# A two-layer kernel on one core: all 16 shared tiles ahead of the routed ones in the first feed-forward layer, batch 1's steps later in attention's prologue

## The chip, the core and the metric

The kernel runs on one core of a Trainium2 chip. That core has a matrix engine (PE in the rows; PEld is its weight load, which overlaps its matmuls), a vector engine (DVE), a scalar engine (ACT), a general engine (POOL) and an engine that mostly starts transfers (SP). "SPq" and "ACTq" in a row are the queues from which SP and ACT start transfers. The metric is the device time of one execution in microseconds (us), as a median of runs.

## What is computed

The input is 2 batches of 1024 tokens with 128 values each. Three residual layers follow one another: a feed-forward layer with a shared expert and seven routed ones of which each token takes two, causal attention with 16 heads of 8 values, and the same feed-forward layer again.

```python
x = x + 0.5 * ffn(layernorm(x))
x = x + attn(layernorm(x))
x = x + 0.5 * ffn(layernorm(x))

def ffn(x):                                     # hidden 352, 7 routed experts
    logits = x @ wr.T + rb
    probs = softmax(logits)
    scores, idx = top_k(probs, 2)
    scores = scores / scores.sum(-1)
    out = expert(x, sg, su, sd)                 # shared
    for e in range(7):
        out = out + w[..., e:e+1] * expert(x, rg[e], ru[e], rd[e])
    return out                                  # expert: silu(x @ g.T) * (x @ u.T), then d

def attn(x):                                    # v = x @ w_v + v_b
    q = (x @ w_q + q_b) @ w_k.T + k_b
    k = x                                       # split into 16 heads of 8
    p = softmax(mask(q @ k.T / sqrt(8)))
    return (p @ v) @ c_proj_w + c_proj_b
```

## The kernel before

**Units of work.** Tokens lie in 16 tiles of 128, and four tiles are a chunk of 512: chunks 0 and 1 are batch 0, chunks 2 and 3 are batch 1. A feed-forward layer does 54 jobs (`NQ`): 16 shared tiles, and 38 routed tiles (`NJ`) whose rows have been sorted by expert. A job takes one step of PE for `up` (L899 to L901: two products of 352 columns, three matmuls each), a step later the transposes of its activations (L919), a step later `down` (L933). ACT does the silu (L1000) and the copy of the transposes (L1008), DVE the product (L1043) and the result (L1079 for a routed tile, L1081 for a shared one).

**The order of jobs** is `JOBS` from `BEFORE`: in the first layer (f = 0) 13 shared tiles, the 38 routed ones, then the last 3 shared ones. POOL sorts: 32 indirect transfers (L1174) write token rows to their places in memory, the first 16 for batch 0 and the next 16 for batch 1, with a short pause (L1184) behind each. SP then loads sorted tiles into the chip (L1260). Routed tiles come in batches (`BATCHES`: tiles 0-1, 2-5, 6-9, 10-11, 12-13, then fours); PE transposes a batch (L953) at the step that `batch_at` names, two steps ahead of its first job where it can. Routed tiles 0 to 9 hold rows of batch 0 alone, so they wait for the first 16 sorts; batch 3 (tiles 10-11) waits for all 32. POOL writes each routed tile's result back to memory (L1197), and after tile 21 batch 0's results are complete and after tile 37 batch 1's.

**Between the layers**, chunk by chunk: load the results (L1271), weigh and add them (ACT L1114 and DVE L1093, L1104 for batch 0; ACT L1126 and POOL L1138 for batch 1), statistics on DVE (L504, L507), four small instructions on POOL for the scale (L515 to L521), the normed rows `z` on ACT (L540), their transposes on PE (L573), a high part on ACT (L579) and a low part on DVE (L585), then the query product `q` on PE (L1508 to L1510 with wq), ACT (L1563, L1565) and DVE (L1571), and the value product `v` on PE (the same lines with wv), ACT (L1543) and POOL (L1553). For batch 0 these steps are placed at steps of the first layer by four hand-written tables: `FRONT_PE`, `BETWEEN_ACT`, `BEHIND_ACT` and `BEHIND_DVE`. "Front" is at the start of the engine's step, "behind" at its end. So `44: (("n_tr", 0),)` puts chunk 0's transposes at the head of PE's step 44. For batch 1 they are placed in attention's prologue by `SECOND_PE` and `SECOND_DVE`, at numbers of ring entries.

**Attention** works on 8 groups of four heads, 4 for each batch. Queries and keys go out to memory in a stacked form (SP L1578) and come back group by group, 5 transfers for one group (L1928 queries, L1936 keys). For each group there are ring entries: 38 blocks of scores (L1605, a mask at L1608 on the diagonal) whose maxima DVE takes (L1757), then a short chain on DVE (L1761, L1763, L1765) and two transposes of the maxima (L1628), which SP puts into the queries (L1949). After that come the exponentials: scores (L1648), exp on ACT (L1816), a mask on POOL (L1863), and the product with the values (L1677). The prologue is the 54 ring entries of `RING_PROLOGUE`: the 38 blocks of group 0, one of group 1, the two transposes, then 13 of group 1. From entry 45 on, score units for the exponentials run among them. Every engine takes its instructions strictly in the order in which they are written, so a wait holds up all that stands behind it on that engine; a ring entry on PE may run four ahead of DVE.

Three key buffers are used in turn. Buffer 2 is cleared by SP (L1421) from memory before group 2 is loaded into it (L1928, L1936); group 2's first block stands in PE's first loop body behind the 24 last blocks of group 1.

The last part of SP's program for the prologue reads in its order (L1977 to L1986):

```python
    for c in range(NCH // 2, NCH):
        keys_sp(K, c)
    for c in range(NCH // 2, NCH):
        queries_sp(K, c)
    rows_load(K, 0, 0, 0, RING_PROLOGUE.index(("mrow", 0, 0)))
    for c in range(NCH // 2, NCH):
        e.wait_ge(K.k_st[c], 16 * 3)
        e.wait_ge(K.q_st[c], 16 * 3)
    keys_clear(K, 2)
    e.wait_ge(K.cleared, keys_cleared(1))
```

## Time and profile before

| what | us |
|---|---|
| median of 3 runs | 570.33 |
| lowest and highest of them | 570.11 and 571.10 |
| the profiled execution, its own time | 571.84 |
| its span, first to last instruction | 570.0 |
| PE busy in it | 521.1 (91%) |
| DVE busy | 388.5 (68%) |
| ACT busy | 319.8 (56%) |
| POOL busy | 272.1 (48%) |

The profiled execution took 571.84 us, of which 570.0 lie between its first and its last instruction. In its trace the first feed-forward layer ends and attention's prologue begins at 162.84 us; the first scores for an exponential start at 199.86 us; the loop over the groups ends near 402 us, and the second feed-forward layer fills the rest. A share of busy time is a mean over stages that are bound by different things, so each stage is read by itself, by what PE waited for last.

### The profile page before, as it was taken

What the parts mean: (1) busy time and instruction counts of PE and PEld (TensorE: products, weight loads), DVE (VectorE), ACT (ScalarE), POOL (GpSimd) and SP (SyncE); (2) the same over time, 40 slices, a digit from 0 to 9 for tenths busy, and PEclk for the clock granted to TensorE, in tenths of its full rate; (3) what the DMA queues carried; (4) which work ended last, traced back from release to release, by engine and by line L of the source; (5) the groups of instructions that cost most, each with busy time, mean ns of one, the idle gap of its engine ahead of it and who ended that gap; (6) DMA issues with size and microseconds to landing.
All of it is one profiled execution on the core that took longest, in us unless ns stands there. A gap on an engine that the chain in (4) does not pass through costs nothing.

```text
span 570.0 us, 11374 instructions
## 1 busy us (share of the span) xinstructions
PE 521.1 (91%) x3574; PEld 406.0 (71%) x3574; DVE 388.5 (68%) x1013; ACT 319.8 (56%) x678; POOL 272.1 (48%) x417
## 2 busy tenths in 40 slices
PE   5985969999996799999999999999999889889995
PEld 2884969998954465656666666565746889889995
DVE  5694635557367888887979888888555775445744
ACT  4552424457444276776767677677776444434643
POOL 8299887667356711212120303030318888854540
PEclk9899789999996899999999999999999999999999
DMA  8922424132861581505050505020001031431414
GB/s 283 294 67 50 111 77 120 45 107 81 242 183 56 170 190 35 173 2 175 2 174 1 176 0 176 1 102 2 2 2 33 31 91 43 118 92 34 125 50 121
DMA packets 41384, 54.65 MB, mean 96 GB/s; under 512 B 6064, under 2 KB 32176, under 8 KB 40560
## 3 DMA queue, kind: packets, MB, share of 16 engines
q1 hardware_dynamic: 32528, 42.70, 26.4%
q0 software_dynamic: 4480, 9.25, 4.9%
q10 hardware_dynamic: 4320, 1.98, 1.3%
q8 instruction: 32, 0.52, 0.4%
q14 instruction: 24, 0.20, 0.1%
HBM read 34.03 MB, written 28.00 MB: 109 GB/s over the span
## 4 chain that ended last, share of the span: by engine, by line
PE 57%; issue 18%; POOL 10%; DMA 6%; DVE 4%; SPq 2%; ACT 2%; ACTq 1%; another core or an unknown queue 1%; POOLq 0%; DVEq 0%
PE psum L1605 11%; PE psum L1648 11%; PE psum L1677 10%; PE psum L933 6%; POOL z_rows L1174 6%; PE psum L919 3%; PE psum L901 3%; PE psum L899 3%; PE psum L900 3%; PE psum L1608 2%; POOL idle L1184 2%; DMA b_p<-in_attn_c_proj_b 2%; DMA yc<-y_rows 1%; DMA y_rows<-ys,to_row 1%; PE psum L1633 1%
## 5 line engine op out<-in xcount | busy, mean ns | idle before, releaser
L1757 DVE TENSOR_REDUCE mxp<-psum 128x1 f32<-128x512 f32 (+3 forms) x304 | 179.0, 654 | 32.9 <-PE psum L1605 32.1
L1816 ACT ACTIVATE probs<-psum 128x512 f32<-128x512 f32 (+1 forms) x304 | 154.9, 578 | 39.8 <-PE psum L1648 37.2
L1863 POOL TENSOR_SCALAR_AFFINE_SELECT probs<-probs 128x512 f32<-128x512 f32 x64 | 40.0, 635 | 174.2 <-ACT probs L1816 174.2
L1648 PE MATMUL psum<-queries,keys 128*128 128x512 f32 (+3 forms) x384 | 122.5, 381 | 0.6 <-DMA queries<-m_rows 0.3
L1605 PE MATMUL psum<-keys,queries 128*128 128x512 f32 (+1 forms) x304 | 116.1, 417 | 2.9 <-DVE mxp L1757 2.4
L1000 ACT ACTIVATE silu<-psum 128x352 f32<-128x352 f32 x107 | 49.6, 463 | 99.5 <-PE psum L901 62.6
L1197 POOL DMA_INDIRECT y_rows<-ys,to_row x76 | 74.3, 977 | 59.1 <-DVE ys L1079 35.4
L1043 DVE TENSOR_TENSOR act<-silu,psum 128x352 f32<-128x352 f32 x107 | 55.6, 519 | 68.0 <-ACT silu L1000 41.7
L933 PE MATMUL psum<-wall_f,at 128*128 (+1 forms) x648 | 92.2, 279 | 2.7 <-DVE x L1081 1.8
L1648 PEld LDWEIGHTS psum<-queries,keys 128*128 128x128 f32 x384 | 66.8, 191 | 26.8 <-ACT probs L1816 12.6
L933 PEld LDWEIGHTS psum<-wall_f,at 128*128 128x128 f32 x648 | 82.1, 194 | 4.1 <-ACT at L1008 2.3
L1605 PEld LDWEIGHTS psum<-keys,queries 128*128 128x128 f32 x304 | 58.1, 194 | 18.1 <-DVE mxp L1757 7.8
L1677 PE MATMUL psum<-probs,vg 128*32 128x512 f32 (+3 forms) x768 | 69.8, 491 | 0.4 <-POOL probs L1863 0.4
L919 PE MATMUL psum<-ident,act 128*128 128x128 f32 x324 | 54.7, 278 | 5.9 <-DVE act L1043 4.4
L899 PE MATMUL psum<-wall,zs_h 128*128 x152 | 56.9, 374 | 1.0 <-issue 1.0
L1008 ACT COPY at<-psum 128x384 f32<-128x384 f32 x108 | 51.3, 475 | 11.0 <-PE psum L919 9.7
L900 PE MATMUL psum<-wall,zs_h 128*128 x152 | 50.4, 331 | 0.0
L901 PE MATMUL psum<-wall,zs_l 128*128 x152 | 50.2, 330 | 0.0
L919 PEld LDWEIGHTS psum<-ident,act 128*128 128x128 f32 x324 | 41.0, 142 | 12.3 <-DVE act L1043 8.2
L1677 PEld LDWEIGHTS psum<-probs,vg 128*32 128x32 f32 x768 | 21.1, 109 | 35.4 <-issue 22.9
L1174 POOL DMA_INDIRECT z_rows<-zrow,slots x32 | 34.4, 1076 | 15.9 <-DVE slots L750 10.5
L1174 POOL DMA_INDIRECT z_rows<-zrow_late,slots x32 | 31.2, 975 | 5.8 <-issue 5.8
(240 smaller groups left out, 732.4 us busy)
## 6 DMA issues: line engine op xcount, KB each, us to landing
z_rows<-q_stack SPq DMA_DIRECT2D x12, 682.5 KB, 5.6
keys<-k_stack SPq DMA_DIRECT2D x32, 128.0 KB, 5.9
queries<-q_stack SPq DMA_DIRECT2D x8, 512.0 KB, 5.3
zg_early<-z_rows SPq DMA_DIRECT2D x44, 65.0 KB
yc<-y_rows SPq DMA_DIRECT2D x10, 256.0 KB, 4.0
zg_late<-z_rows SPq DMA_DIRECT2D x32, 65.0 KB
k_stack<-zt_h SPq DMA_DIRECT2D x8, 256.0 KB, 2.9
q_stack<-q_h SPq DMA_DIRECT2D x8, 256.0 KB, 3.7
```

Source lines behind the costliest of these rows:

```text
L899: e.matmul(dst, zh, weight(K.wall, base, hi, HID), start=True, stop=False)
L900: e.matmul(dst, zh, weight(K.wall, base, lo, HID), start=False, stop=False)
L901: ins = e.matmul(dst, zl, weight(K.wall, base, hi, HID), start=False, stop=True)
L919: ins = e.transpose(bank(K, at_bank(f, q))[:, k * P:(k + 1) * P], K.act[:, q % 2, k * P:(k + 1) * P], K.ident[:, :])
L933: ins = e.matmul(bank(K, Y_BANK)[:, 0:EMB], K.at[:, q % 2, k * P:(k + 1) * P], weight(K.wall_f, base, DN + k * EMB, EMB), start=(k == 0), ...
L1174: e.indirect_dma_start(K.z_dram[f], bass.IndirectOffsetOnAxis(ap=K.slots[:, g:g + 1], axis=0), K.zrow[f][:, t, :], None).then_inc(K.z_sc[t ...
L1197: e.indirect_dma_start(K.y_dram[f], bass.IndirectOffsetOnAxis(ap=K.to_row[:, j:j + 1], axis=0), K.ys[:, j % RING_Y, :], None).then_inc(K.y ...
L1605: ins = e.matmul(dst, K.queries[u][:, i * P:(i + 1) * P], K.keys[u][:, heads[0]:heads[-1] + 1, k0 * P:(k0 + nb) * P], start=True, stop=Tru ...
L1648: ins = e.matmul(slot(K, u, d, n)[:, m * (q1 - q0):(m + 1) * (q1 - q0)], K.keys[v][:, j, kt * P:(kt + 1) * P], K.queries[v][:, q0:q1], sta ...
L1677: ins = e.matmul(bank(K, O_BANK)[32 * j:32 * j + 32, q0 - half * CHUNK:q1 - half * CHUNK], K.vg[:, kt, j, :], probs_of(K, n)[:, j, :], sta ...
L1757: e.tensor_reduce(K.mxp[:, heads[0]:heads[-1] + 1, i, which], scores, AX.X, ALU.max).then_inc(K.A["taken"], 1)
L1816: e.activation(probs_of(K, product)[:, heads[0]:heads[-1] + 1, :], src, ACT.Exp, scale=SCALE).then_inc(K.A["ex"], 1)
```

## The change

The functions are the same ones, in another order, with a few waits and banks that follow from it.

- **Jobs of the first layer.** All 16 shared tiles come first, the 38 routed ones behind them. `batch_at` now transposes batch 3 (routed tiles 10-11) one step ahead of its first job, not two. The second layer's jobs stay as they are.
- **Batch 0's steps.** Mixing, statistics, transposes and queries move three steps down the tables, so they stand at the same routed tile as before; the exceptions are chunk 1's transposes (step 47 to 49), its query product (48 to 50) and ACT's and DVE's part of it. The normed rows of chunks 0 and 1 are made by DVE (steps 44 and 47, "behind"), where ACT made them. Values of chunks 0 and 1 go from steps 50 and 51 to entries 0 and 2 of the prologue.
- **Batch 1's steps** go to later entries of the prologue: transposes of chunk 2 from entry 19 to 25, of chunk 3 and the queries of chunk 2 from 24 to 30, queries of chunk 3 from 29 to 35, values from 30 and 32 to 36 and 38.
- **Transfers.** SP stores the queries of chunk 1 in two parts, the first four heads (all that group 0 needs) first, loads group 0, then stores the other twelve. Keys of batch 1 are stored from ACT's queue. SP's stores of the queries of batch 1 come behind `rows_load` of group 0.
- **POOL.** The four additions of the projection's bias (L2060) leave the place before attention's loop: two come ahead of `v_bias_pool(0)`, two go into the first loop bodies.

```diff
-BEFORE = (13, 11)
+BEFORE = (TT, 11)
-ONE_AT_AGAIN = (43, NQ)
+ONE_AT_AGAIN = (46, NQ)
-        if step == BEFORE[f] + j - (min(b, 2) if f == 0 else 1 if j == WHOLE else 2):
+        if step == BEFORE[f] + j - min(2 if f else b, 1 if j == WHOLE else 2):
-    return c != 1 if k == 0 else k == 1 or c == 2
+    return c != 1 if k == 0 else c >= 2 if k == 1 else c == 2
 def v_pe(K, c):
     if c == 0:
-        e.wait_ge(K.A["qf"], 1)
+        e.wait_ge(K.A["qf"], 2)
     elif c == 1:
-        e.wait_ge(K.A["qf"], 2)
+        e.wait_ge(K.FF[0]["yev"], NQ)
-SECOND_PE = {19: (("n_tr", 2),), 24: (("n_tr", 3), ("q", 2)), 29: (("q", 3),), 30: (("v", 2),), 32: (("v", 3),)}
-SECOND_DVE = {13: (("n_stats", 2),), 16: (("n_stats", 3),), 20: (("n_lo", 2),), 26: (("n_lo", 3),)}
+SECOND_PE = {0: (("v", 0),), 2: (("v", 1),), 25: (("n_tr", 2),), 30: (("n_tr", 3), ("q", 2)), 35: (("q", 3),), 36: (("v", 2),),
+             38: (("v", 3),)}
+SECOND_DVE = {18: (("n_stats", 2),), 21: (("n_stats", 3),), 26: (("n_lo", 2),), 32: (("n_lo", 3),)}
 def attn_pool(K):
+            if (p, u) in ((0, 1), (0, 2)):
+                proj_bias_pool(K, u + 1)
 def attn_sp(K):
-    for c in range(NCH // 2):
-        keys_sp(K, c)
-        queries_sp(K, c)
+    keys_store(K, e, 0)
+    queries_sp(K, 0)
+    keys_store(K, e, 1)
+    queries_sp(K, 1, (0, 4))
...
     keys_load(K, 0, 0, 0)
-    for c in range(NCH // 2):
-        e.wait_ge(K.q_st[c], 16 * 3)
+    e.wait_ge(K.q_st[0], 16 * 3)
+    e.wait_ge(K.q_first, 16 * 3)
+    queries_load(K, 0, 0, 0)
+    queries_sp(K, 1, (4, HEADS))
     e.wait_ge(K.FF[0]["mix"], 4)
-    queries_load(K, 0, 0, 0)
     keys_load(K, 0, 0, 1)
+    e.wait_ge(K.q_st[1], 16 * 3)
     queries_load(K, 0, 0, 1)
-    for c in range(NCH // 2, NCH):
-        keys_sp(K, c)
+    rows_load(K, 0, 0, 0, RING_PROLOGUE.index(("mrow", 0, 0)))
     for c in range(NCH // 2, NCH):
         queries_sp(K, c)
-    rows_load(K, 0, 0, 0, RING_PROLOGUE.index(("mrow", 0, 0)))
-FRONT_PE = {10: (("places", 1),), 44: (("n_tr", 0),), 45: (("q", 0),), 47: (("n_tr", 1),), 48: (("q", 1),),
-            50: (("v", 0),), 51: (("v", 1),)}
+FRONT_PE = {10: (("places", 1),), 47: (("n_tr", 0),), 48: (("q", 0),), 49: (("n_tr", 1),), 50: (("q", 1),)}
         @block.scalar
+            v_act(K, 0)
+            v_act(K, 1)
             weigh_both_act(K, 2)
...
             q_act(K, 2)
+            keys_store(K, e, 2)
             q_act(K, 3)
+            keys_store(K, e, 3)
         @block.gpsimd
+            e.wait_ge(K.NS[1]["z"], 2)
+            proj_bias_pool(K, 0)
+            proj_bias_pool(K, 1)
             v_bias_pool(K, 0)
             v_bias_pool(K, 1)
...
-            proj_bias_pool(K)
             attn_pool(K)
```

How instructions stand at three places, before and after. Lines of the changed kernel are numbered 1 to 4 higher here for the same statement (L1079 has become L1080, L1757 has become L1760).

DVE near the end of the first layer, where chunk 1 has been mixed (`x<-x,yc`); `act` is the product of a job, `ys` a routed result, `stats` the statistics of chunk 1. Before:

```order
L1093 SCALAR_TENSOR_TENSOR x<-yc,w,x 128x128 x4
L1104 TENSOR_TENSOR x<-x,yc 128x512
L1043 TENSOR_TENSOR act<-silu,psum 128x352
L1079 COPY ys<-psum 128x128
L504 BN_STATS stats<-x 128x6 x4
L507 BN_AGGR mv<-stats 128x2 x4
```

After:

```order
L1094 SCALAR_TENSOR_TENSOR x<-yc,w,x 128x128 x4
L1105 TENSOR_TENSOR x<-x,yc 128x512
L553 TENSOR_SCALAR z<-x,mv,rstd 128x128 x4
L1044 TENSOR_TENSOR act<-silu,psum 128x352
L1080 COPY ys<-psum 128x128
L505 BN_STATS stats<-x 128x6 x4
L508 BN_AGGR mv<-stats 128x2 x4
```

The four instructions that make chunk 0's normed rows `z` now stand between the mixing and the next job's product.

SP in attention's prologue; `q_stack` and `k_stack` are the stacked queries and keys in memory, `m_rows` the maxima of group 0, `keys<-q_stack` the clearing of key buffer 2, and the rows behind it group 2's load. Before:

```order
L1578 DMA k_stack<-zt_l 16x8x512
L1578 DMA k_stack<-zt_h 16x8x512
L1578 DMA q_stack<-q_h 16x8x512 x2
L1578 DMA q_stack<-q_l 16x8x512
L1578 DMA q_stack<-q_h 16x8x512 x2
L1578 DMA q_stack<-q_l 16x8x512
L1949 DMA queries<-m_rows 4x8x128 x2
L1421 DMA keys<-q_stack 32x4096 x4
L1928 DMA queries<-q_stack 128x1024
L1936 DMA keys<-k_stack 32x1024 x4
```

After:

```order
L1942 DMA keys<-k_stack 32x1024 x4
L1934 DMA queries<-q_stack 128x1024
L1955 DMA queries<-m_rows 4x8x128 x2
L1579 DMA q_stack<-q_h 16x8x512 x2
L1579 DMA q_stack<-q_l 16x8x512
L1579 DMA q_stack<-q_h 16x8x512 x2
L1579 DMA q_stack<-q_l 16x8x512
L1422 DMA keys<-q_stack 32x4096 x4
L1934 DMA queries<-q_stack 128x1024
L1942 DMA keys<-k_stack 32x1024 x4
```

The four rows of stores of batch 1's queries stood ahead of `m_rows` and now stand between it and the clearing; those of batch 1's keys are gone from SP.

PE in the prologue around the transposes of chunk 2 (the first `ident,z`) and of chunk 3 (the second), with the query product of chunk 2 (`wq`). Before:

```order
L1605 MATMUL psum<-keys,queries 128x512 x2
L573 MATMUL psum<-ident,z 128x128 x4
L1605 MATMUL psum<-keys,queries 128x512 x4
L1608 MATMUL psum<-ident_b,mask_b 128x512
L1605 MATMUL psum<-keys,queries 128x512
L573 MATMUL psum<-ident,z 128x128 x4
L1508 MATMUL psum<-zt_h,wq_h 128x512
L1509 MATMUL psum<-zt_l,wq_h 128x512
L1510 MATMUL psum<-zt_h,wq_l 128x512
```

After:

```order
L1607 MATMUL psum<-keys,queries 128x512 x2
L574 MATMUL psum<-ident,z 128x128 x4
L1607 MATMUL psum<-keys,queries 128x512 x5
L1610 MATMUL psum<-ident_b,mask_b 128x512
L574 MATMUL psum<-ident,z 128x128 x4
L1509 MATMUL psum<-zt_h,wq_h 128x512
L1510 MATMUL psum<-zt_l,wq_h 128x512
L1511 MATMUL psum<-zt_h,wq_l 128x512
```

The pieces read alike; 6 more ring entries (`keys,queries`) stand ahead of the first of them, 25 instead of 19.

## Rows read from the trace of the kernel before

**Rows 1.** The page's second part: 40 equal slices of the span, 14.25 us each.
```profile
PE   5985969999996799999999999999999889889995
```
**Rows 2.** Waits of PE up to 260 us: total, times, longest.
```profile
PE psum L1628 <- DVE mm_hl L1765: 3.5, 1, 3.5
```
**Rows 3.** Busy time by stage: stretch, its length, each engine, then PEclk, DMA share, GB/s.
```profile
57.90:77.40 19.50, 19.44 (x128) 19.05 (x128) 12.71 (x42) 8.06 (x19) 17.52 (x26) 0.86 0.34 85
163.00:200.00 37.00, 26.54 (x96) 15.69 (x96) 31.93 (x69) 14.22 (x33) 21.73 (x31) 0.82 0.40 121
```
**Rows 4.** Timeline: start, length, engine, line, work [idle before and its releaser]; first wait.
```profile
51.13 0.96 POOL L1174 DMA_INDIRECT z_rows<-zrow,slots  x1 [0.17 <-issue]
...
56.44 0.50 PE L953 MATMUL psum<-ident,zg_early 128*128 128x128 f32 x2 [4.90 <-DMA zg_early<-z_rows]
```
**Rows 5.** The same timeline, second wait, and two successive jobs at full clock.
```profile
82.05 0.66 PE L953 MATMUL psum<-ident,zg_early 128*128 128x128 f32 x2 [4.67 <-DMA zg_early<-z_rows]
...
95.16 0.41 PE L899 MATMUL psum<-wall,zs_h 128*128 x1
...
97.12 0.41 PE L899 MATMUL psum<-wall,zs_h 128*128 x1
```
**Rows 6.** Timeline of PE behind the step of chunk 1's mixing; L552's four instructions on DVE.
```profile
132.94 0.55 PE L919 MATMUL psum<-ident,act 128*128 128x128 f32 x3 [0.66 <-DVE act L1043]
...
L552 DVE TENSOR_SCALAR zrow<-x,mv,rstd x4: 314/342/343, 10.8 to 11.5; 128x128 f32<-128x128 f32 x4
```
**Rows 7.** Timeline of the last jobs and of group 0's load, with that load's landing.
```profile
148.07 0.69 DVE L1571 TENSOR_TENSOR q_l<-q_f,q_h 128x512 fp32r<-128x512 f32 x1 [0.44 <-ACT q_h L1565]
149.51 0.31 PE L1508 MATMUL psum<-wv_h,zt_h 128*128 128x128 f32 x1
150.88 0.38 PE L899 MATMUL psum<-wall,zs_h 128*128 x1
154.95 0.34 SPq L1928 DMA_DIRECT2D queries<-q_stack  x1
...
162.84 0.48 PE L1605 MATMUL psum<-keys,queries 128*128 128x512 f32 x1
DMA to landing us min/median/max: 4.4/4.4/4.4
```
**Rows 8.** Timeline of batch 1's results, from the last routed tile to chunk 2's transposes.
```profile
158.39 0.29 DVE L1079 COPY ys<-psum 128x128 f32<-128x128 f32 x1
168.73 5.32 POOL L1138 TENSOR_TENSOR x<-x,yc 128x512 f32<-128x512 f32 x4 [5.47 <-ACT yc L1126]
...
177.85 1.09 PE L573 MATMUL psum<-ident,z 128*128 128x128 f32 x4 [3.09 <-issue]
```
**Rows 9.** Prologue: DVE's first maxima, POOL's value biases, the maxima's chain over all groups.
```profile
163.70 7.33 DVE L1757 TENSOR_REDUCE mxp<-psum 128x4 f32<-128x512 f32 x13
...
L1553 POOL TENSOR_TENSOR v_all<-v_all,b_v 128x128 f32<-128x128 f32 x16 | 6.7, 456 | 0.0
L1763 DVE CAST mm_hl<-nmax x8: 180/520/1192, 193.9 to 399.4; 128x32 fp32r<-128x32 f32 x8
L1765 DVE TENSOR_TENSOR mm_hl<-nmax,mm_hl x8: 192/193/1195, 195.1 to 399.7; 128x32 fp32r<-128x32 f32 x8
```
**Rows 10.** Timeline of SP with the times to landing, and group 2's first block on PE.
```profile
188.12 1.24 SPq L1578 DMA_DIRECT2D q_stack<-q_h  x2
...
198.59 1.71 SPq L1421 DMA_DIRECT2D keys<-q_stack  x4
211.03 1.82 SPq L1936 DMA_DIRECT2D keys<-k_stack  x4
q_stack<-q_h SPq DMA_DIRECT2D x8, 256.0 KB, 3.7
keys<-k_stack SPq DMA_DIRECT2D x4, 128.0 KB, 4.9
...
221.86 0.40 PE L1605 MATMUL psum<-keys,queries 128*128 128x512 f32 x1
```

64 lines of the change are left out of this document (32 added, 32 removed).

## The prediction

> **What bounds the kernel now.** Read first PE's line in the 40 slices [rows 1]. From the 15th slice on it stands at 9 through the loop over the groups: there nothing but PE sets the pace, and an earlier start of the loop moves the end by as much. The low digits lie before it: slices 4 and 6 (43 to 57 us and 71 to 86 us) and slices 13 and 14 (171 to 200 us). The change works on just these places, so each is read for what PE waits for last.
>
> In the first layer PE waits twice for sorted rows. It stands idle for 4.90 us before the transposes at 56.44 [rows 4], which wait for SP's load, which waits for the 16th sort, issued by POOL at 51.13. It stands idle for 4.67 us before those at 82.05 [rows 5], which need all 32 sorts. POOL's pace and not PE's sets both moments. What PE does in the meantime is free. Behind the first wait the granted clock is low: 0.86 as a mean from 57.9 to 77.4 us, where PE is busy for 19.44 of 19.50 us [rows 3]; since the clock knows only two levels, 1.2 and 2.4 GHz, some 5 us of that stretch ran at the lower.
>
> In the prologue from 163 to 200 us, PE is busy for 26.5 us of 37 and DVE for 31.9 [rows 3], so DVE's maxima and the chain that brings batch 1's rows share the bound. Two waits of PE show which: 3.09 us before chunk 2's transposes at 177.85 [rows 8], and 3.5 us for the maxima's chain [rows 2].
>
> **Shared tiles first.** A job at full clock takes 1.96 us on PE (97.12 less 95.16, [rows 5]). PE reached the first wait at 56.44 - 4.90 = 51.54. Three more jobs fill it to 57.4, 1 us behind the rows' arrival, so this wait goes entirely, and with it the half clock behind it. About 0.5 us of transposes and 1 us until ACT and DVE have split the rows remain, then come nine jobs (nine, because batch 3's transposes now stand one step later) and eight more transposes: 58.9 + 9 x 1.96 + 0.8 = 77.3 us. That is where PE stood before, at 82.05 - 4.67 = 77.38, with eight routed jobs done. What is late next is therefore the second wait, and I take it unchanged: POOL's 32 sorts depend on nothing that moves. At 82.05 the kernel has done 25 jobs instead of 21. Everything behind is 4 x 1.96 = 7.8 us shorter for PE. The routed tiles are only one job earlier, 2.0 us.
>
> **Values out of the layer.** Twelve matmuls of chunk 0's values take 150.88 - 149.51 = 1.37 us [rows 7], chunk 1's the same: -2.7 us for the layer. They come back in the prologue, chunk 0's ahead of the first ring entry (+1.4), chunk 1's behind the second, under DVE's maxima.
>
> **Rows normed by DVE.** Four instructions on DVE cost 11.5 - 10.8 + 0.34 = 1.1 us [rows 6]. For chunk 0 they stand between the mixing and the next job's product, and just there PE already waits 0.66 us for that product [rows 6]. DVE is late in this step, so I take the whole 1.1 us as a delay of PE; it would be nothing if the results came earlier than I think. For chunk 1 the four stand in a step in which DVE waits for rows anyway: nothing. Taking them off ACT gives PE nothing, as it didn't wait for them. Chunk 1's transposes and queries one step earlier make ACT's and DVE's steps crowded: +0.3, between 0 and 1.
>
> PE ends the layer at 162.84 - 7.8 - 2.7 + 1.1 + 0.3 = 153.7 us.
>
> **Group 0's load.** With chunk 0's values PE is at 155.1 before the first ring entry. The low part of chunk 1's queries was done at 148.07 + 0.69 = 148.76 and the load had landed at 154.95 + 4.4 = 159.35 [rows 7], 10.6 us later; PE came only at 162.84, so it did not see this. Now the queries are earlier by one job, by one step and later by the 1.1 us: 148.76 - 2.0 - 2.0 + 1.1 = 145.9. With the old distance the load lands at 156.5. The first part stores only four of sixteen heads and so should be quicker; keys and queries of group 0 still have to come, so 154.3 is the least I allow. I take 155.5, nearer the upper end than half way since the 4.4 us of the last load remain. The first ring entry moves by 155.5 - 162.84 = -7.3 us.
>
> **Batch 1's chain.** It starts at the last routed result, at 158.39 + 0.29 = 158.68 before. This one now is the last job of the layer, so it ends about 0.5 us behind PE, at 154.2: -4.5 us. From there results go to memory, come back, are weighed, added and normed, and chunk 2's transposes follow at 177.85, 19.2 us later [rows 8]. One thing is added on POOL: the value biases of chunks 0 and 1 (8 instructions, about 3.4 us by [rows 9]) now wait for ACT, whose copies stand behind its wait for the results' store. They end some 0.8 us after the addition at 168.73 - 4.5 = 164.2 could start (nothing if ACT is early, 2 us if late). Chunk 2's transposes: 177.85 - 4.5 + 0.8 = 174.1. Ahead of them stand 25 ring entries instead of 19; DVE took 7.33 us for 13 [rows 9], 0.56 each, and its first one starts 0.9 us behind PE's, at 156.4, so with some 2.5 us of statistics and a wait of 0.8 us for the added rows it has done 25 at 156.4 + 14.1 + 2.5 + 0.8 = 173.8. The chain and the ring now meet at about the same moment, and the 3.09 us of waiting is used up. Before, entry 37 was done about 0.3 us before 193.9 [rows 9], 15.8 us after the transposes; six entries fewer stand between, so 15.8 - 6 x 0.56 = 12.4, and DVE begins the last chain at 186.5 instead of 193.6: -7.1 us.
>
> **The maxima's chain.** Its cast and subtraction took 1.19 and 1.20 us for group 0, against a median of 0.52 and 0.19 over the groups [rows 9], while POOL added the projection's bias beside them, the additions that the change takes away. Their place is taken by value biases of 0.456 us each [rows 9]. The gain lies between 0 and 1.7 us; I take 1.2, nearer the upper end because these instructions are a third as long. The Trainium skill (SBUF — State Buffer, "Who interferes with whom") says that a DVE instruction with two inputs in SBUF, or a cast in a two-port mode, and a POOL instruction exclude each other for a whole instruction; the rows of this chain agree, and by it each of the two would wait for one bias at most, so the gain would be at least 1.19 + 1.20 - 0.52 - 0.19 - 2 x 0.46 = 0.8 us, an estimate. The first scores for an exponential so start at 199.86 - 7.1 - 1.2 = 191.6.
>
> **Stores behind `rows_load`.** Here SP pays. Six stores (two took 1.24 us, so 3.7 in all, and 3.7 to land, [rows 10]) now stand between the maxima's rows and the clearing of key buffer 2, where there was nothing. At least the moving of 1.5 MB remains, which I put at 6.5 us; the delay is 6.5 to 7.4. The clearing took from 198.59 to 210.6, group 2's load lands at 211.03 + 1.4 + 4.9 = 217.3, and PE's first block of group 2 stands at 221.86 [rows 10]: 4.6 us to spare. So PE will wait there for 6.6 - 4.6 = 2.0 us, 0 to 4 with what other transfers do to it. PE bounds the loop, so this is lost in full. The keys' stores on ACT (3.7 us of issuing) end before ACT is needed for exponentials; two bias additions in the loop stand on POOL, which is idle for most of it. Both nothing, or up to 0.5 us together.
>
> **Sum.** 7.1 + 1.2 - 2.0 = 6.3 us off the profiled execution's 571.84. That one lies 1.5 us above the median of the runs, and the change doesn't touch the difference: 570.33 - 6.3 = 564.0 us.
>
> **Rivals.** (a) *Group 2 is not missed.* The stores are partly done before the clearing must start, or the clearing is quicker than 12 us since nothing else runs: 564.0 - 2.0 = 562.0. For it: DMA is mostly idle in these stages (0.40, [rows 3]). (b) *Group 0's load is late*: the queries' chain keeps its 10.6 us and gains only the 2.0 of the routed tiles. First entry at 148.76 - 2.0 + 1.1 + 10.6 = 158.5, a wait of 3.4 us and a half clock behind it. The whole prologue slides by 2 to 3 us: 566.5. (c) *Group 2 costs more*, 5 us instead of 2, as clearing and stores meet: 567. (d) *DVE holds up the layer*: the normed rows wait on DVE for POOL, where the scale stands behind a scatter, and jobs queue behind them. 1.5 us more: 565.5. (e) *The change doesn't do what it says*: rows of the first batch still come after PE. They came at 56.4 and PE comes at 57.4; below 1 us of delay it costs nothing, beyond that one for one, so with rows 2.5 us later than before the time is that of (d). (f) *Slower*: the wait for group 2 grows until it eats everything. PE would stand for so long that the clock falls behind it as it did behind the 4.90 us wait; the eight jobs behind it took 19.5 us [rows 3] where 8 x 1.96 + 0.8 = 16.5 would do, 3.0 more. To come out above 570.33 + 1.1 the wait has to exceed 8.3 + 1.1 - 3.0 = 6.4 us, so group 2's rows must land 4.4 us later than I expect. Clearing and stores would have to stretch each other by 40% of the clearing's 12 us. (g) *Nothing moves*, within 0.2%: the same with a wait of 5 to 6.4 us, or (b) and (c) together.
>
> **How the numbers follow.** Forecast 0.42; (a) 0.18; (b) 0.14; (c) 0.10; (d) with (e) 0.07; (f) 0.05; (g) 0.04. Faster by over 0.2%: 0.91; within 0.2%, about what a measurement can tell from no change: 0.04; slower: 0.05. The range leaves out (f), (g) and the outer half of (b) and (c), and reaches down to (a) with 1.5 us for a chain of batch 1 that is quicker: 560.0 to 568.0 us.
>
> **What would show it.** PE's waits in the first layer: one of about 4.7 us at 82 us instead of two, and no half clock between 58 and 77 us. PE's first ring entry near 155.5 us; if it is at 158, (b). Chunk 2's transposes near 174 with less than 1.5 us of waiting. Cast and subtraction below 1 us each. The first exponential's scores near 191.6. Then a wait of PE for `queries<-q_stack` or `keys<-k_stack` about 22 us later; if it is missing, (a). I would be wrong altogether if the second wait in the first layer grew, since POOL's sorts were slower, or if the loop ran slower than before per group.

## The result, and the profile after

Faster by 0.9%: a median of 566.9 us over 13 runs (564.05 to 569.78) against 571.74 us over 13 runs of the kernel before (569.71 to 574.8), ratio 0.991, 95% interval 0.9884 to 0.9935. The forecast was 564.0 us against a before of 570.33, ratio 0.989. The size is near; half of the reasons are not. The profiled execution of after took 569.66 us (span 567.8; before 571.84 and 570.0). It is one of the slower ones of its kernel: the spans differ by 2.2 us, the medians by 4.8. One run of e11 below, of 1270.4 us, fell in a slow state and is left out of its median. Both kernels' runs spread over some 5 us, so the experiments below are read mainly in their traces, place by place.

The 40 slices of after, to be held against [rows 1]. The 5 in slice 4 has become an 8 and the 6 in slice 6 a 7, slices 13 and 14 (7 and 8) stand where 6 and 7 stood, and a new 7 is in slice 16, inside the loop over the groups. Slices 9, 10 and 12 are an 8 instead of a 9:

```profile
PE   5898879988987897999999999999999889899995
PEclk9899999999976997999999999999999999999998
```

Timeline of PE and DVE in after (start, length, engine, line, work, idle time before and its releaser):

```profile
60.48 0.42 PE L900 MATMUL psum<-wall,zs_h 128*128 x1 [1.66 <-DVE zs_l L1068]
...
82.21 0.41 PE L954 MATMUL psum<-ident,zg_early 128*128 128x128 f32 x2 [2.87 <-DMA zg_early<-z_rows]
...
126.59 0.55 PE L920 MATMUL psum<-ident,act 128*128 128x128 f32 x3 [1.49 <-DVE act L1044]
...
132.93 0.55 PE L920 MATMUL psum<-ident,act 128*128 128x128 f32 x3 [1.64 <-DVE act L1044]
...
154.25 0.31 PE L1509 MATMUL psum<-wv_h,zt_h 128*128 128x128 f32 x1
...
157.16 0.50 PE L1607 MATMUL psum<-keys,queries 128*128 128x512 f32 x1 [1.38 <-DMA queries<-q_stack]
...
161.43 0.69 DVE L1760 TENSOR_REDUCE mxp<-psum 128x4 f32<-128x512 f32 x1 [2.21 <-PE psum L1607]
...
175.99 1.09 PE L574 MATMUL psum<-ident,z 128*128 128x128 f32 x4 [1.23 <-issue]
...
187.94 0.25 DVE L1764 TENSOR_REDUCE nmax<-mxp 128x32 f32<-128x96 f32 x1
188.23 0.18 DVE L1766 CAST mm_hl<-nmax 128x32 fp32r<-128x32 f32 x1
188.45 0.19 DVE L1768 TENSOR_TENSOR mm_hl<-nmax,mm_hl 128x32 fp32r<-128x32 f32 x1
...
218.03 0.77 PE L1607 MATMUL psum<-keys,queries 128*128 128x512 f32 x1 [3.58 <-DMA keys<-k_stack]
```

Read down. The 4.90 us wait of [rows 4] is gone; 1.66 us for the rows' split remain. The second wait ends when it ended before, at 82.21 against 82.05 [rows 5]. The layer ends at 154.25. The first ring entry comes at 157.16 instead of 162.84 [rows 7], the last maxima's chain starts at 187.94 instead of 193.6, and its cast and subtraction take 0.18 and 0.19 us. Then PE stands idle for 3.58 us in front of group 2. Busy time in stretches of after (length, engines, then PEclk, DMA share, GB/s):

```profile
158.00:165.00 7.00, 7.00 (x25) 5.22 (x24) 4.61 (x8) 1.07 (x2) 3.15 (x8) 0.51 0.89 248
172.00:182.00 10.00, 8.11 (x22) 5.61 (x23) 9.02 (x22) 4.53 (x11) 5.03 (x11) 0.50 0.00 0
192.00:196.00 4.00, 3.60 (x17) 2.67 (x18) 3.44 (x7) 3.04 (x7) 1.01 (x2) 1.00 0.94 295
196.00:198.00 2.00, 2.00 (x15) 1.83 (x14) 2.00 (x4) 1.98 (x5) 0.64 (x1) 1.00 0.62 201
216.00:218.00 2.00, 0.00 (x0) 0.00 (x1) 0.19 (x1) 0.00 (x0) 0.00 (x0) 0.55 0.15 35
218.00:222.00 4.00, 3.97 (x10) 2.65 (x10) 2.08 (x3) 1.44 (x4) 0.00 (x0) 0.50 0.00 0
222.00:224.00 2.00, 2.00 (x16) 1.67 (x19) 0.88 (x2) 1.25 (x4) 0.64 (x1) 0.74 0.00 0
```

Here is the new 7 of slice 16: no work from 216 to 218, then half clock until some 223 us. The first row is another half clock that was not foreseen, over the values of chunk 1. The second row's half clock is not new: before has one from 173 to 183 us.

**Places of the balance.** Start times (us) in the profiled executions: end of PE's second wait for sorted rows; end of DVE's copy of the last routed result; first ring entry; chunk 2's transposes; the maxima's chain (`nmax`); the first scores for an exponential; SP's third issue of the maxima's rows (`rows_load`); and the distance between the last two. The kernels e1 to e12 are those of the experiments.

| kernel | 2nd wait ends | last routed | ring entry 1 | chunk 2 | `nmax` | first scores | 3rd rows | distance |
|---|---|---|---|---|---|---|---|---|
| before | 82.1 | 158.68 | 162.84 | 177.85 | 193.62 | 199.86 | 255.8 | 55.9 |
| after | 82.2 | 154.83 | 157.16 | 175.99 | 187.94 | 192.40 | 254.2 | 61.8 |
| after again (e11) | none | 153.63 | 156.01 | 174.59 | 185.42 | 189.90 | 250.7 | 60.8 |
| e1 stores ahead | 83.1 | 155.38 | 158.18 | 177.49 | 188.88 | 195.78 | 253.0 | 57.2 |
| e2 values together | 81.5 | 153.79 | 155.93 | 175.01 | 186.55 | 191.01 | 249.7 | 58.7 |
| e3 shared last | 82.1 | 154.07 | 159.61 | 176.47 | 188.10 | 192.56 | 253.6 | 61.0 |
| e4 norm on ACT | 83.7 | 154.62 | 156.42 | 175.77 | 187.34 | 191.79 | 252.6 | 60.8 |
| e5 stores on ACT | 81.8 | 154.88 | 156.32 | 175.95 | 187.13 | 192.87 | 250.1 | 57.3 |
| e6 e3 and e5 | 81.2 | 151.50 | 157.03 | 173.91 | 185.26 | 192.35 | 249.7 | 57.4 |
| e7 bias back | 80.8 | 153.44 | 155.05 | 174.91 | 185.72 | 190.19 | 250.2 | 60.0 |
| e8 batch 3 later | 81.4 | 156.92 | 157.76 | 177.68 | 188.52 | 193.00 | 254.2 | 61.2 |
| e9 clear split | 82.1 | 154.56 | 156.53 | 175.21 | 187.07 | 191.55 | 249.1 | 57.5 |
| e10 values in layer | 82.0 | 156.57 | 156.38 | 175.50 | 187.43 | 191.91 | 251.2 | 59.3 |
| e12 less behind | 83.6 | 155.85 | 157.02 | 176.57 | 188.29 | 193.39 | 249.7 | 56.3 |

Before to after: 7.5 us are won up to the first scores, 5.9 are lost in the last column, 1.6 are left. In e11, the same kernel, it is 10.0, 4.9 and 5.1, which is nearer to what the medians differ by. The experiments ask what made either number.

Two stretches scatter by themselves. Behind the second wait the clock was at 0.5 for 3 us or more in most executions (before from 80.5 to 87.3 us, after from 83 to 86.5) and not at all in e4, e6 and e11. And every kernel has a half clock around chunk 2's transposes. It lasted some 3 us beyond their start in e7, e8 and e11 and 4.4 to 6.1 us in the other changed kernels; from the transposes to `nmax` it is 10.8 us in those three and 11.2 to 12.0 in the others. So about 1 us in the columns from `nmax` on can be the clock alone.

### The profile page after: what moved, and what is told of

It is laid out like the page before. It is cut to its first block, busy times and chain, and to the rows that moved or that the text cites. A ratio compares the mean times of both kernels' runs of the same rounds, so it can differ in the third digit from the quotient of the medians.

```text
span 567.8 us, 11380 instructions
## 1 busy us (share of the span) xinstructions
PE 521.3 (92%) x3574; PEld 406.8 (72%) x3574; DVE 389.0 (69%) x1021; ACT 317.0 (56%) x670; POOL 272.2 (48%) x413
## 4 chain that ended last, share of the span: by engine, by line
PE 56%; issue 20%; DMA 10%; DVE 6%; SPq 5%; ACT 1%; ACTq 1%; DVEq 0%
PE psum L1607 11%; PE psum L1650 10%; PE psum L1679 9%; PE psum L934 6%; PE psum L920 3%; PE psum L902 3%; PE psum L900 3%; PE psum L901 3%; PE psum L1610 2%; DMA b_p<-in_attn_c_proj_b 2%; DVE mxp L1760 2%; DMA keys<-q_stack 2%; SPq L1261 2%; DMA q_stack<-q_l 1%; SPq L1254 1%
## 5 line engine op out<-in xcount | busy, mean ns | idle before, releaser
L1760 DVE TENSOR_REDUCE mxp<-psum 128x1 f32<-128x512 f32 (+3 forms) x304 | 179.3, 656 | 41.5 <-PE psum L1607 33.6
L1607 PE MATMUL psum<-keys,queries 128*128 128x512 f32 (+1 forms) x304 | 117.5, 423 | 6.9 <-DMA keys<-k_stack 3.6
L934 PEld LDWEIGHTS psum<-wall_f,at 128*128 128x128 f32 x648 | 81.5, 193 | 3.7 <-ACT at L1009 1.7
L1607 PEld LDWEIGHTS psum<-keys,queries 128*128 128x128 f32 x304 | 59.6, 199 | 23.0 <-DVE mxp L1760 6.9
L900 PE MATMUL psum<-wall,zs_h 128*128 x152 | 55.9, 368 | 1.7 <-DVE zs_l L1068 1.7
L901 PE MATMUL psum<-wall,zs_h 128*128 x152 | 49.5, 326 | 0.0
```

What stands on the lines that cost most here:

```text
L900: e.matmul(dst, zh, weight(K.wall, base, hi, HID), start=True, stop=False)
L901: e.matmul(dst, zh, weight(K.wall, base, lo, HID), start=False, stop=False)
L934: ins = e.matmul(bank(K, Y_BANK)[:, 0:EMB], K.at[:, q % 2, k * P:(k + 1) * P], weight(K.wall_f, base, DN + k * EMB, EMB), start=(k == 0), ...
L1607: ins = e.matmul(dst, K.queries[u][:, i * P:(i + 1) * P], K.keys[u][:, heads[0]:heads[-1] + 1, k0 * P:(k0 + nb) * P], start=True, stop=Tru ...
L1760: e.tensor_reduce(K.mxp[:, heads[0]:heads[-1] + 1, i, which], scores, AX.X, ALU.max).then_inc(K.A["taken"], 1)
```

## Experiments: what the loss is

**e1, all stores ahead of `rows_load`, as before the change**

```diff
-    rows_load(K, 0, 0, 0, RING_PROLOGUE.index(("mrow", 0, 0)))
     for c in range(NCH // 2, NCH):
         queries_sp(K, c)
+    rows_load(K, 0, 0, 0, RING_PROLOGUE.index(("mrow", 0, 0)))
```

> The changed kernel with one thing put back: SP issues the six stores of chunks 2's and 3's queries ahead of `rows_load` and not behind it. Theory 1 (the stores behind `rows_load` start the clearing of key buffer 2 too late): the clearing starts near 194 us instead of 198.04, PE's wait of 3.58 us for group 2's keys at 218.03 is gone, and so is the half clock from 217 to 223 us that took another 2.2 us. The stores cost the maxima's rows at most 1 us, since the low part of chunk 3's queries is ready at 187.9 us and three issues of 0.6 us end at 189.7, where `rows_load` begins anyway. 566.9 - 5.8 + 1 = about 562 us, 561 to 564. Rival 1 (transfers, not SP's order, are short: the clearing takes 12.6 us and group 2's load 7 us whatever stands before them, and the clearing only starts 1 us earlier because the stores land later): the wait stays above 2 us, 566 us. Rival 2 (the stores' transfers fall on the maxima's rows): PE's wait for the maxima's rows grows from 1.59 us to 4 us or more, first scores for an exponential after 194.5 us, 564.5 us.

568.36 us, ratio 0.9954 (0.9927 to 0.9981): not better than after. PE and SP in e1:

```profile
195.78 0.55 PE L1650 MATMUL psum<-queries,keys 128*128 128x512 f32 x1 [4.04 <-DMA queries<-m_rows]
...
188.86 2.07 SPq L1579 DMA_DIRECT2D q_stack<-q_h  x2
191.30 1.15 SPq L1579 DMA_DIRECT2D q_stack<-q_l  x1
192.61 1.24 SPq L1955 DMA_DIRECT2D queries<-m_rows  x2
```

Theory 1 is right about group 2 (no wait; the distance is 57.2) and wrong about the price ahead of it, where the numbers of rival 2 came (4.04 us, 195.78), but not mainly by its transfers. Chunk 3's stores start at 188.86 us, three issues take 3.6 us there instead of 1.9, and the rows leave 2.84 us later than after's 189.77, of which 0.9 was there at `nmax`. From their issue to the first scores it is 3.2 us instead of 2.6; that 0.5 is the transfers' part. So the place of the stores is a trade and not an oversight.

**e5, chunk 3's stores issued by ScalarE, chunk 2's ahead**

```diff
+    queries_sp(K, 2)
     rows_load(K, 0, 0, 0, RING_PROLOGUE.index(("mrow", 0, 0)))
-    for c in range(NCH // 2, NCH):
-        queries_sp(K, c)
...
             v_act(K, 3)
+            queries_sp(K, 3, e=e)
```

> The changed kernel with chunk 2's three query stores ahead of `rows_load` on SP, and chunk 3's three issued by ScalarE behind its copies of the values, beside `rows_load` and not behind it. What e1 showed: the stores ahead of `rows_load` delay its issue by 2.84 us, their transfers alone by no more than 0.5 us. Theory 1 (SP's order is the price of both places): `rows_load` stays at 189.8 us, the scores for an exponential at 192.4 to 192.9, the last store lands near 194.5 instead of 198.0 us, the clearing begins there, group 2 lands 3.5 us earlier and PE waits for it by less than 0.3 us, without a half clock behind it: 561.5 us, 560 to 563.5. Rival 1 (transfers): with stores beside the maxima's rows, those land 1.5 us or more later, 564.5 us. Rival 2 (ScalarE): three issues ahead of the first exponential push its table load and the exponential by 1 us or more, 563.5 us. Rival 3 (the wait for group 2 is no loss, because PE is ahead of ScalarE and VectorE there and would wait for them instead): the wait is gone and the next groups' maxima's rows start no earlier than 223.6, 254.2 and 283.7 us; 566.9 us.

565.47 us, ratio 0.9916 (0.9885 to 0.9947). PE in e5:

```profile
192.87 0.47 PE L1650 MATMUL psum<-queries,keys 128*128 128x512 f32 x1 [2.88 <-DMA queries<-m_rows]
...
194.00:197.00 3.00, 3.00 (x11) 2.72 (x10) 2.52 (x5) 2.24 (x5) 0.61 (x1) 0.50 0.67 158
```

SP issued the rows at 188.95, in time, and yet PE waited 2.88 us for them instead of 1.59: 1.3 us (rival 1), of which 0.4 is the issue itself (1.56 us for 1.19) and the rest the transfers. No wait for group 2 follows, distance 57.3, and that includes the half clock of the second row, which stands behind the wait for the maxima's rows. The trace is 4 us better than after's at the third rows, but only 0.6 better than e11's; the median of the runs is 1.4 lower, the ratio not lower at all (0.9916 against 0.991).

**e9, the clearing in two halves; e11, the changed kernel again, on the same chip**

```diff
     for c in range(NCH // 2, NCH):
         queries_sp(K, c)
+    keys_clear(K, 2, 0)
     for c in range(NCH // 2, NCH):
         e.wait_ge(K.k_st[c], 16 * 3)
         e.wait_ge(K.q_st[c], 16 * 3)
-    keys_clear(K, 2)
+    keys_clear(K, 2, 2)
```

> The changed kernel with the clearing of key buffer 2 in two halves: its parts 0 and 1 (which only the full-precision queries of chunks 2 and 3 used, read for the last time at 187.9 us) are cleared right behind the issues of the stores, without waiting for their landing; parts 2 and 3 behind it, as the whole clearing did. Nothing that stands ahead of `rows_load` is touched. Theory 1 (PE's wait for group 2 is the end of stores, clearing and load in a row): the second half starts near 199 us and lands 6 us later, near 205.5 instead of 210.6, group 2's keys land near 213, 5 us ahead of 218.0; PE doesn't wait there, no half clock follows, and from the first scores for an exponential to the third issue of the maxima's rows it takes 57 us (e1, e5 and e6: 57.2 to 57.35) instead of 58.7 to 61.8 (the changed kernel, e2, e3, e4, e7, e8): 563.2 us, 562 to 565. Rival 1 (the transfers share one bandwidth: stores, clearing and the maxima's rows are moved in the same total time, in whatever order): the second half lands at 208 us or later, PE waits 1 to 2.5 us and a half clock may follow, 565.5 us. Rival 2 (the half clock comes anyway, as in e5 behind the wait for the maxima's rows): no wait for group 2 and yet 59 us, 565 us.

> The changed kernel itself, once more, beside e9 and e10. Theory 1 (how long the half clock behind the wait for group 2 lasts differs from one execution to the next, and the profiled one of the changed kernel, with 6.8 us of it, was the dearest of six kernels with that wait): from the first scores for an exponential to the third issue of the maxima's rows 58.7 to 61.2 us instead of 61.8, the wait itself 2.5 to 3.8 us as before, and the profiled execution 1 to 4 us below 569.66. Rival (the loss is fixed): 61.8 us again. Median 566.9 us, 565.5 to 568.

e9: 566.43 us, ratio 0.989 (0.9853 to 0.9927). e11: 569.8 us, ratio 0.9938 (0.9903 to 0.9973), with a before of 574.64. Side by side e9 is 3.4 us faster, with intervals that overlap. Stretches of e9 and its PE at group 2:

```profile
192.00:196.00 4.00, 4.00 (x22) 2.99 (x21) 3.72 (x7) 3.87 (x9) 0.65 (x1) 1.00 1.01 321
196.00:200.00 4.00, 4.00 (x29) 2.86 (x31) 3.90 (x8) 3.57 (x7) 1.88 (x3) 1.00 1.04 264
200.00:206.00 6.00, 6.00 (x53) 3.14 (x46) 4.67 (x10) 2.76 (x5) 0.00 (x0) 1.00 0.97 208
...
215.24 0.47 PE L1607 MATMUL psum<-keys,queries 128*128 128x512 f32 x1 [1.62 <-DMA keys<-k_stack]
```

Rival 1 is right here: the DMA engines are at a share of 1.0 from 192 to 206 us. Splitting only closes the gap that after has at 196 to 200 us (share 0.62); what remains is bytes. The wait of 1.62 us was followed by no half clock, and the distance fell to 57.5. In e11 the wait was 3.43 us, with clock 0.50 from 216 to 218 us, and the distance 60.8. Over the seven profiled executions with all stores and the whole clearing behind `rows_load` (after, e11, e2, e3, e4, e7, e8) the wait was 2.5 to 3.8 us and the distance 58.7 to 61.8; e2, with 2.73 us of waiting and the clock at 1.0 behind it, is the 58.7. e10, also of this kind, had 3.34 us, no half clock and 59.3. The 57.2 to 57.5 of e1, e5, e6 and e9 are not free of such a price: e9 has its 1.62 us, and the other three a half clock of some 3 us right behind the first scores (PE had waited 2.9 to 4.0 us for the maxima's rows). Before and e12, with neither, have 55.9 and 56.3. Against 56.3 the wait costs 2.4 and 3.0 us where no half clock follows (e2, e10), a little less than itself, and 3.7 to 5.5 us where one does, 1.1 to 1.9 more than itself.

**e12, fewer bytes behind `rows_load`**

```diff
+    e.wait_ge(K.NS[1]["z"], 3)
+    keys_clear(K, 2, 1, 2)
+    queries_sp(K, 2)
     rows_load(K, 0, 0, 0, RING_PROLOGUE.index(("mrow", 0, 0)))
-    for c in range(NCH // 2, NCH):
-        queries_sp(K, c)
+    queries_sp(K, 3)
+    keys_clear(K, 2, 0, 1)
...
-    keys_clear(K, 2)
+    keys_clear(K, 2, 2, 4)
```

> The changed kernel with less left to move behind `rows_load`: part 1 of key buffer 2, which nothing uses, is cleared when chunk 2's rows are normed (about 175 us, where the 16 DMA engines stand still), chunk 2's query stores go ahead of `rows_load`, chunk 3's and the clearing of part 0 behind it, and parts 2 and 3 behind the stores' landing. In e9 the DMA engines were busy without a break from 192 to 206 us with 3.5 MB and group 2 still came 1.62 us late. Theory 1 (bytes behind `rows_load` set group 2's load): 0.75 MB of stores and 1.5 MB of clearing remain, which at the 215 GB/s of e9 is 10.5 us instead of 16; group 2's queries are issued near 203 to 204.5 us, its keys land near 211, PE doesn't wait and has no half clock there; chunk 2's stores, issued at 184 and landed at 190, cost the maxima's rows 0 to 1 us. From the first scores for an exponential to the third issue of the maxima's rows 56 to 57.3 us; ratio to the kernel before 0.984, 0.981 to 0.988, some 562.5 us against a before of 571. Rival 1 (stores ahead of `rows_load` cost what they save, as in e1 and e5): PE's wait for the maxima's rows grows from 1.6 to 2.9 us or more, with a half clock behind it, ratio 0.989. Rival 2 (the clearing of part 1 meets batch 1's results): chunk 2's transposes later than 95 us behind the second wait for sorted rows, ratio 0.991.

565.81 us, ratio 0.989 (0.9855 to 0.9926). Group 2's queries were issued at 203.74 us, PE did not wait there, the clock stayed at 1.0, distance 56.3, all as theory 1 said. The price ahead was 0.6 us, counted from `nmax` to the first scores, and no half clock stood there:

```profile
193.39 0.47 PE L1650 MATMUL psum<-queries,keys 128*128 128x512 f32 x1 [2.23 <-DMA queries<-m_rows]
```

The ratio that was expected (0.984) did not come. In this trace the third rows are 4.5 us earlier than in after although the second wait ended 1.4 us later. Of that gain the medians show 1.1 us, or 2.7 if the ratio is held against e11's, within the intervals; against e11's trace it is 1.1 us too. From the third rows to the end the profiled executions differ by up to 4 us (311.1 us in e2, 315.3 in e12, 313.6 in after), in code that no experiment touches, but for two bias additions that e7 takes out; that is as much as what is looked for.

## Experiments: what the gain is

**e3, the shared tiles 13 first and three last**

```diff
-BEFORE = (TT, 11)
+BEFORE = (13, 11)
```

and every step of `FRONT_PE`, `BETWEEN_ACT`, `BEHIND_ACT` and `BEHIND_DVE` from 42 on, with `ONE_AT_AGAIN`, three lower.

> The changed kernel with 13 shared tiles ahead of the routed ones and three behind them, as before, and every step that hangs on the routed tiles three jobs earlier; values, norm on VectorE, biases and stores as in the changed kernel. Theory 1 (more shared tiles first fill POOL's first wait): PE waits 4.9 us near 56 us again and again has a half clock behind it, 21 jobs are done at 82 us instead of 25, and the layer ends 7 to 8 us later, near 162 us; batch 1's last result comes only 2 us later. The first ring entry moves from 157.2 to 163.5, the first scores for an exponential from 192.4 to 197 to 198.5; 571.5 us, 570 to 573. Rival (POOL's sorts alone set the pace, so that the order of the tiles only moves the waiting from one place to the other): layer's end within 2 us of 154.3, 567 to 568 us.

564.46 us over 4 runs, ratio 0.9886 (0.9845 to 0.9927): not slower than after, as far as 4 runs tell. PE in e3:

```profile
56.83 0.66 PE L954 MATMUL psum<-ident,zg_early 128*128 128x128 f32 x2 [3.32 <-DMA zg_early<-z_rows]
...
158.23 0.30 PE L1509 MATMUL psum<-wv_h,zt_h 128*128 128x128 f32 x1
...
159.61 0.44 PE L1607 MATMUL psum<-keys,queries 128*128 128x512 f32 x1
...
176.47 0.87 PE L574 MATMUL psum<-ident,z 128*128 128x128 f32 x3 [1.48 <-issue]
```

The first wait is back, with a half clock from 56 to some 62 us, and the layer ends 4.0 us later (158.23 against 154.25; neither theory's number), and nearly nothing comes of it: the first scores start at 192.56 against 192.40. Where it goes is seen on POOL and DVE between the layers. POOL adds batch 1's results (`x<-x,yc`) and then takes chunk 2's statistics (`mv`) into the scale. In after, in e3 and in e2 below:

```profile
166.96 5.34 POOL L1139 TENSOR_TENSOR x<-x,yc 128x512 f32<-128x512 f32 x4 [1.17 <-ACT yc L1127]
172.27 0.23 POOL L516 TENSOR_SCALAR var_e<-mv 128x4 f32<-128x4 f32 x1
...
165.16 5.34 POOL L1139 TENSOR_TENSOR x<-x,yc 128x512 f32<-128x512 f32 x4
172.76 0.23 POOL L516 TENSOR_SCALAR var_e<-mv 128x4 f32<-128x4 f32 x1 [2.26 <-DVE mv L508]
...
168.72 0.87 DVE L505 BATCH_NORM_STATS2 stats<-x 128x6 f32<-128x128 f32 x4 [1.75 <-POOL x L1139]
```

Two chains meet here: batch 1's results and DVE's maxima, 18 of which stand ahead of the statistics. In after they meet within 0.3 us: the statistics are ready at 172.03, POOL's additions end at 172.30. In e3 the results are earlier (additions end at 170.50; the last routed result is 0.8 us earlier, since the three tiles behind it are shared ones, and the loads took 4.3 us to land instead of 5.5), and POOL waits 2.26 us for DVE. So there the later end of PE's work is felt, but it has shrunk. DVE starts its maxima 2.4 us later, at 160.3 us, and then loses only 0.7 us up to the 18th where after loses 2.4, since the clock stays at 1.0 from 158 to 165 us. What is left is 0.6 us at the statistics and 0.5 at chunk 2's transposes. The headline of the change, worth 4 us at the layer's end, is worth 0.2 at the first scores.

**e6, the order of e3 with the stores of e5**

> The stores as in e5 and the shared tiles as in e3 (13 first, three last). e3 came out at the changed kernel's time or below it. Theory 1 (the order of the shared tiles brings nothing, the stores are what the changed kernel loses): layer's end near 158.3 us and yet the first scores for an exponential within 0.7 us of e5's, no wait for group 2, and the time within 1.5 us of e5's. Rival (the shared tiles first are worth the 4 us by which the layer ends earlier, which e3's runs hid by chance): 3 us or more above e5.

565.04 us, ratio 0.9894 (0.9861 to 0.9928), against e5's 565.47: theory 1. Two pairs, (after, e3) and (e5, e6), say the same. In the second the shared tiles last are even 1.9 us ahead at `nmax`, in part because e6 has no half clock behind its second wait and e5 has one, and most of it goes again in the cast and in a longer wait for the maxima's rows (3.60 us).

**e8, batch 3's transposes two jobs ahead again**

```diff
-        if step == BEFORE[f] + j - min(2 if f else b, 1 if j == WHOLE else 2):
+        if step == BEFORE[f] + j - (min(b, 2) if f == 0 else 1 if j == WHOLE else 2):
```

> The changed kernel with the transposes of batch 3 of the first layer two jobs ahead of their first job again instead of one. Theory 1 (the transposes' place decides how many routed jobs stand ahead of the second wait for sorted rows): PE comes to that wait one job earlier, near 77.4 us, waits 4.7 us instead of 2.9, and every later job of the layer and the last routed result come 1.97 us later; the first ring entry and chunk 2's transposes too, 568.8 us. Rival (another wait of 1 us or more in the layer takes it up, as the mixing's at 124 us, where VectorE waits 1.98 us for results): less than 1 us, 567.5 us.

```profile
81.36 0.66 PE L954 MATMUL psum<-ident,zg_early 128*128 128x128 f32 x2 [4.72 <-DMA zg_early<-z_rows]
```

4.72 us of waiting instead of 2.87, and the last routed result 2.1 us later (156.92), though the wait ended 0.8 us earlier; chunk 2's transposes 1.7 us later, first scores 0.6, or 1.4 counted from the wait's end; 1.1 us between these two places is the shorter half clock named above. Theory 1 in the trace. In the runs (566.93 us, 0.9926, 0.9898 to 0.9955) it can't be told from after.

**e10, values of chunks 0 and 1 in the layer**

```diff
-SECOND_PE = {0: (("v", 0),), 2: (("v", 1),), 25: ...
+SECOND_PE = {25: ...
-... 50: (("q", 1),)}
+... 50: (("q", 1),), 51: (("v", 0), ("v", 1))}
```

with ScalarE's copies at step 51 and banks and waits as before the change.

> The changed kernel with the 24 matmuls of the values of chunks 0 and 1 ahead of the layer's last shared tile again (both at step 51) and out of the prologue. Counted from the end of PE's second wait for sorted rows (82.2 us). Theory 1 (values in the layer push the last routed result and so batch 1's chain, which sets the prologue): the last routed result ends 2.7 us later than 72.6 us behind that wait, the first ring entry no later than now, since its load was waited for, and the first scores for an exponential come 1 to 2.5 us later than 110.2 us behind the wait: 568.5 us. Rival (values are worth nothing where they stand: 1.4 us ahead of the first ring entry and 2.65 us at half clock behind entry 1 are given back in full): within 0.5 us of 110.2, 566.9 us.

570.79 us, ratio 0.9951 (0.992 to 0.9982), beside e11's 0.9938 in the same comparison. The last routed result is 1.7 us later, but chunk 2's transposes and the first scores are 0.5 us earlier: the rival. The 1.7 us are eaten by the way of batch 1's results. Landing times of the four loads of `yc` behind the first layer (min, median, max), in after:

```profile
L1272 ACTq DMA_DIRECT2D yc<-y_rows x4: 422/528/530, 159.6 to 161.2; - x4
...
DMA to landing us min/median/max: 4.9/5.5/5.9
```

and in e10:

```profile
L1272 ACTq DMA_DIRECT2D yc<-y_rows x4: 393/528/531, 161.1 to 162.7; - x4
...
DMA to landing us min/median/max: 3.0/3.7/4.6
```

Issued 1.5 us earlier, they landed beside group 1's keys and queries and chunk 1's other stores (DMA share 0.89 from 158 to 165 us) and took 1.8 us longer. That is the extreme: in e11, the same kernel, the median is 4.5 us, and in the other kernels with loads issued at 156 to 162 us it is 4.2 to 5.1.

**e2, both values ahead of the first ring entry**

```diff
-SECOND_PE = {0: (("v", 0),), 2: (("v", 1),), 25: ...
+SECOND_PE = {0: (("v", 0), ("v", 1)), 25: ...
```

> The changed kernel with the twelve matmuls of chunk 1's values moved from behind ring entry 1 to ahead of ring entry 0, next to chunk 0's. Theory 1 (chunk 1's values cost DVE time, since at half clock they took 2.65 us and DVE waited 2.21 us for the next scores): they fill PE's wait of 1.38 us for group 0's queries, the clock stays at 1.0 up to the first maxima, the first ring entry stays at 157 to 157.6 us, DVE begins its run of maxima some 2 us earlier than 162.3 us and the first scores for an exponential come 1 to 2 us before 192.40: 565.4 us. Rival (batch 1's chain sets chunk 2's transposes at 175.99 us, so that DVE's 2 us are only waited away there): transposes at 175.5 to 176 with a wait above 2 us, first scores for an exponential within 0.5 us of 192.4, 566.9 us.

566.28 us, ratio 0.9925 (0.9895 to 0.9955). The wait of 1.38 us and the half clock at 158 us are gone and DVE idled 2.5 us instead of 4.2, but PE then waited 2.27 us for chunk 2's rows, and DVE 1.75 us for the additions ahead of the statistics (last row of the fence in e3): with the half clock gone, batch 1's results are what comes last. The first scores are 1.4 us earlier, of which 1.0 had been there at the last routed result: the rival. In six executions in which PE waited at most 1.0 us ahead of its first ring entry or not at all (e4, e5, e7, e8, e9, e12) the clock stayed at 1.0 too; where it had waited 1.38 to 1.84 us (after, e11, e1) it fell.

**e4, chunks 0 and 1 normed by ScalarE**

```diff
-    return c != 1 if k == 0 else c >= 2 if k == 1 else c == 2
+    return c != 1 if k == 0 else k == 1 or c == 2
```

with `n_z` at 45 and 47 in `BEHIND_ACT` and out of `BEHIND_DVE`.

> The changed kernel with the rows of chunks 0 and 1 normed by ScalarE again, a job later than they stood on VectorE by the same distance from the mixing as before. Theory 1 (the four instructions on VectorE delay the product of the next job, which PE waits for): PE's two waits for VectorE's product at 126.6 and 132.9 us (1.49 and 1.64 us) fall to about 0.7 us each, the layer ends 1 us earlier than 154.25 and the first ring entry comes up to 1 us earlier, if the queries follow; 566.0 us. Rival (the queries' chain, not PE's jobs, sets the first ring entry, and ScalarE's norm puts it later): the layer's end moves but group 0's load lands 0.5 to 1 us later, 567 to 567.5 us.

566.23 us, ratio 0.9933 (0.9903 to 0.9964). In e4:

```profile
126.67 0.55 PE L920 MATMUL psum<-ident,act 128*128 128x128 f32 x3 [1.62 <-DVE act L1044]
...
132.02 0.55 PE L920 MATMUL psum<-ident,act 128*128 128x128 f32 x3 [0.65 <-DVE act L1044]
```

Only the second of the two waits shrinks, from 1.64 to 0.65 us, to [rows 6]'s 0.66. The norm on VectorE costs 1.0 us of the layer, as predicted; the first wait belongs to the mixing's load. From the second wait's end to the last routed result e4 takes 1.7 us less than after, but it also has no half clock behind that wait. The runs don't show the 1.0 us.

**e7, the projection's bias back ahead of the loop**

```diff
             v_bias_pool(K, 3)
+            e.wait_ge(K.NS[1]["z"], NCH)
+            for c in range(NCH):
+                proj_bias_pool(K, c)
```

> The changed kernel with the four additions of the projection's bias back on POOL behind chunk 3's value bias, ahead of the loop over the groups, as before. Theory 1 (a cast and a subtraction of VectorE wait for POOL's addition beside them): the cast and the subtraction of the maxima's chain take 1.0 to 1.3 us each instead of 0.18 and 0.19 us, the chain ends 1.7 to 2.1 us later than 188.64 us counted from its last maximum, the first scores for an exponential likewise, 568.8 us. Rival (in the changed kernel the chain stands earlier than POOL's additions, since chunk 3's value bias ends only at 191.8 us, so that the additions no longer meet it): cast and subtraction stay at 0.2 us, the time at 566.9 us, and the move of the biases is worth nothing by itself.

563.69 us over 4 runs, ratio 0.9888 (0.9848 to 0.9927): no loss. POOL and DVE in e7:

```profile
184.40 1.28 POOL L1146 TENSOR_TENSOR q_l<-q_f,q_h 128x512 fp32r<-128x512 f32 x1 [2.00 <-ACT q_h L1566]
186.24 3.38 POOL L1552 TENSOR_TENSOR v_all<-v_all,b_v 128x128 f32<-128x128 f32 x8 [0.57 <-ACT v_all L1542]
189.58 5.01 POOL L2062 TENSOR_TENSOR x<-x,b_p 128x512 f32<-128x512 f32 x4
...
186.01 0.18 DVE L1766 CAST mm_hl<-nmax 128x32 fp32r<-128x32 f32 x1
186.22 0.19 DVE L1768 TENSOR_TENSOR mm_hl<-nmax,mm_hl 128x32 fp32r<-128x32 f32 x1
```

(The additions are taken out of their two other places.) The rival, with a reason of its own: the cast lies in POOL's idle 0.57 us ahead of the value biases, and the subtraction begins 0.02 us before the first of them; in after it is the same. In the kernel before it fell among the additions:

```profile
192.57 4.93 POOL L2060 TENSOR_TENSOR x<-x,b_p 128x512 f32<-128x512 f32 x4
...
193.90 1.19 DVE L1763 CAST mm_hl<-nmax 128x32 fp32r<-128x32 f32 x1
195.13 1.20 DVE L1765 TENSOR_TENSOR mm_hl<-nmax,mm_hl 128x32 fp32r<-128x32 f32 x1
```

Each of those four takes 1.23 us; they end near 193.8, 195.0 and 196.3, and VectorE's two instructions end at 195.09 and 196.33. And in e6 the cast met the subtraction of chunk 3's queries:

```profile
185.22 1.27 POOL L1146 TENSOR_TENSOR q_l<-q_f,q_h 128x512 fp32r<-128x512 f32 x1 [3.12 <-ACT q_h L1566]
...
185.55 0.98 DVE L1766 CAST mm_hl<-nmax 128x32 fp32r<-128x32 f32 x1
186.56 0.19 DVE L1768 TENSOR_TENSOR mm_hl<-nmax,mm_hl 128x32 fp32r<-128x32 f32 x1
```

POOL ends at 186.49, the cast at 186.53. So the mechanism (each waits for the end of the POOL instruction beside it) is shown three times, and the move of the biases is not what removed it: the chain's place among POOL's instructions did. What made the idle 0.57 us is plain only in part: ScalarE now issues the keys' stores, and its copies of the values, which the biases wait for, come later. That wasn't tried by itself, and neither were the later ring entries of batch 1's steps, so their share of the gain is not shown.

## Why the prediction was right or wrong

- **Waits of the first layer: right.** One wait instead of two, 25 jobs done by the second wait's end, no half clock between 58 and 77 us, end at 82.2 as taken. PE was 2.0 us later at that wait than said (79.34 for 77.3), 1.2 of it from the first 50 us; it cost nothing.
- **PE's end of the layer: right**, 154.25 for 153.7. Undone one at a time, its terms are not all as large as taken: three shared tiles 4.0 us (three jobs of the four, taken as 5.9; e3), batch 3's place 2.1 and values 1.7, both at the last routed result (2.0; e8, and 2.7; e10), norm 1.0 the other way (1.1; e4). They don't add up to the 8.6 us that were won. One more piece was in no term: the half clock behind the second wait lasted to 87.3 us before and to 86.5 in after.
- **What follows from it: the meeting point right, the gain on the way to it wrong.** The prediction carried the layer's end into the ring by way of group 0's load (-7.3 us; measured -5.7, the queries' stores and load taking 10.6 us as before and not 9.6), and said that the ring and batch 1's chain then meet at about the same moment. They do, within 0.3 us in after. But it let DVE run through its first 25 maxima without a loss to a half clock. Against e3, PE's 4.0 us are 2.4 at DVE's first maximum, as PE now waits 1.38 us for group 0's load, and the half clock behind that wait takes 1.7 of these. And with wait and half clock gone (e2: DVE's third maximum 3.6 us earlier, 157.85 for 161.43) batch 1's chain comes last, and the first scores gain 0.4 us, the 1.0 us of the last routed result counted off. So neither of the two alone was worth much, and the prediction took the three shared tiles for part of the gain, though it had itself noted that they bring the routed tiles nothing.
- **Batch 1's chain: 1.9 us short.** Transposes at 175.99 for 174.1. The last routed result ends at 154.82 for 154.2. The failed term is 'From there results go to memory, come back': 19.2 us from the last routed result, and 21.2 in after. All of the 2.0 us lies ahead of the weighing, 1.7 of it in the landing (5.5 us for 3.8); in e11 the landing is 4.5 us and the whole 21.0. That chunk 2's statistics began on DVE only at 170.75 us, 1.2 us after its additions, cost next to nothing, as POOL was busy with chunk 3's until 172.30. The value biases, priced 0.8, stood on the same stretch (POOL waited 1.17 us behind them for ScalarE), so they cost nothing.
- **Values 'under DVE's maxima': wrong.** At half clock they took 2.65 us and DVE idled 2.21. By e2 it cost the first scores some 0.4 us and no more, as batch 1's chain came at the same time.
- **Maxima's chain: the direction right, the size above its range (2.0 us for 1.2, at most 1.7), the cause wrong**, by e7. The Trainium skill (SBUF — State Buffer, "Who interferes with whom") says that whichever of the two engines issues first holds the shared ports for its whole instruction; the three pairs of end times above agree. What decides is then the moment, and the prediction should have asked where in POOL's row the chain would fall.
- **First scores for an exponential: 192.40 for 191.6.** Near by luck in part: 1.4 us too late at `nmax`, 0.6 too early behind it.
- **Stores behind `rows_load`: the mechanism right, the size a third.** Taken 2.0 us; 5.9 in the profiled execution, 2.8 to 5.9 over eight traces against the 55.9 of before. Two pieces are missing. 'PE will wait 2.0 us': it was 3.6 in after and 2.5 to 3.8 in others. Counted from the first scores, the clearing started 6.9 us later than before (6.6 taken, on an estimate of 6.5 us for 1.5 MB that no row gives), it took 12.5 us for 12.1, and the load behind it 7.0 us for the 6.3 of the sum. And behind the wait a half clock for up to 6 us, which the prediction priced in its rival (f) alone and not in the forecast. A wait of 2 us next to a clock that falls behind idle PE has two prices.
- **The sum**: -7.1 - 1.2 + 2.0 became -5.7 - 1.8 + 5.9 in the profiled execution, -1.6 at the third rows. Other executions lose 1 to 3 us less in the last term. In e11, the same kernel, the sum is -8.2 - 1.8 + 4.9 = -5.1, beside medians 4.8 apart. That the forecast's 6.3 is near to it is in part luck: in e11 a loss put 2.9 us too small met a gain put 1.7 too small, and that gain differs by 2.5 us between two executions of one kernel.

The gains of e5, e9 and e12 at the third rows, 4 to 5 us against after's profiled execution, shrink to 1 to 3.5 in the medians. Most of it is that this execution was a dear one: against e11's they are 0.6, 1.6 and 1.1 us. What is left is inside the scatter of what follows, and it stays open how much these three are worth.

## To carry to other kernels

Before you count an earlier start, follow it to the next meeting point, and ask what each of the chains that meet there keeps of it: here 4 us less of PE's work in the layer were 2.4 us at DVE's first maximum, 0.6 at its statistics, and 0.2 at the first scores. A transfer that leaves earlier leaves into other traffic, so take its landing time from a stretch with the same DMA share. And price a new wait of the bound engine twice, with and without the half clock behind it.

## What was not expected of the hardware

- A wait of 2.5 to 3.8 us was followed by clock 0.50 in six profiled executions and by 1.0 in two. At nearly the same wait (3.58 us in after, 3.34 in e10) the distance in the table's last column was 61.8 and 59.3 us.
- Three issues of 256 KB stores on SP took 1.9 us in after (193.18 to 195.06) and 3.6 us in e1 (188.86 to 192.45), where ScalarE was issuing stores of its own until 189.9. A gap of 0.4 us between two issues is part of the 3.6; that ScalarE's queue is the reason was not tried.
- The clearing's 2 MB kept the 16 DMA engines at a share of 1.0 with only 208 GB/s (e9, 200 to 206 us); with stores among it (192 to 196 us) the same share moved 321 GB/s.
